# First pass over a graph's matrix: rows read in quarters and turned in place by VectorE, in place of a turned copy kept in HBM

## The chip, the cores and the metric

The kernel runs on one core of one Trainium2 chip. The metric is the device time of one execution in microseconds (us). All arithmetic is fp32, apart from one product that the kernel before does in two fp32r pieces.

## What is computed

`adj` is a 5120 x 5120 fp32 matrix A (105 MB), `x` a 5120 x 64 fp32 matrix. Cut to what matters:

```python
e  = par0 * par1 * (diag[:, None] * x @ W) + x          # W, diag, par: first 2048 rows / other 3072 rows
h  = A @ (A.T @ e)                                       # layer 0: one product with A.T, one with A
x0 = layernorm(x + layernorm(h) * gamma + beta + x)
x1 = layernorm(x0 + (1 - 0.1 * x0 - 0.01 * sum(x0 * (A @ x0))))          # layer 1
deg = clip(rowsum(A) + 1, 1)                                              # layer 2
z  = concat([x1, (A @ x1 + x1) / deg]) @ W2 + b2;  x2 = layernorm(x1 + relu(z) / norm(relu(z)))
t1 = A @ x2;  t2 = 2 * A @ t1 - x2;  t3 = 2 * A @ t2 - t1                 # layer 3
out = layernorm(x2 + x2 @ W3[0] + t1 @ W3[1] + t2 @ W3[2] + t3 @ W3[3] + b3)
```

So there is one product with the transposed matrix (u = A.T e) and six with A itself (h, layer 1, layer 2, t1, t2, t3), each of 64 columns. A does not fit in the on-chip memory (SBUF); each product streams blocks of it.

## The kernel before, in words

A is cut into 10 x 10 blocks of 512 x 512 (1 MB each; `BLK`, `NB`). TensorE contracts over partitions. A product with A.T can use a block as it lies in HBM (128 rows of A on the partitions, four such tiles to a block); a product with A needs the block turned.

**First stage (L501 to L561 on TensorE, L433 to L453 on ScalarE, L768 to L796 on VectorE).** For each block column j, SyncE loads the ten blocks (i, j) as they lie (`load`, L342; five buffers `nat`; runs of 512 elements, 2 KB). TensorE turns each block with 16 transposes (L539), ScalarE copies the four results from PSUM into `at_raw` (L447) and stores the turned block to a scratch tensor in HBM, `a_transposed` (L430, one megabyte, 8 KB to a partition). TensorE adds the block's part of u (L551, eight matmul records of 64 columns a block) and, one block column late, the block's part of h: ScalarE rounds the turned block to fp32r (`at_hi`, L425), VectorE forms the rest (`at_lo`, L740), and TensorE multiplies both with the split u (L509). VectorE adds up the rows of each natural block for `deg` (L765) and the parts of h into `part` (L751). So when the first stage ends, u and nearly all of h are there, and 100 MB have been read and 100 MB written.

**The sweeps (`multiply_block`, L621 to L665).** The five other products run as "sweeps" s = 0 to 4, with 5 for the tail (`SWEEPS = 6`). The rows of a product can be finished in one order and the next product started in the other, so that one loaded block serves the end of product s-1 and the beginning of product s at once: `BOTH` blocks have 128 columns of weights, two vectors side by side; `BEGIN` and `END` blocks 64 columns for one of the two. The list `blocks` holds 332 of them: 55 BEGIN in sweep 0; 42 BOTH, 13 BEGIN and 3 END under each of sweeps 1 to 4; 45 END in the tail. The last block column of h comes between the stage and sweep 0, in `last_h_part` (L667). Sixteen slots hold turned blocks (`at_raw` 10, `at_more` 6); a plan made when the program is built gives each block a slot, and SyncE issues the 291 loads (L378) in order, each behind a wait for the block that last used its slot. TensorE's order is written out: between the halves of a block (`mid`) it turns the finished rows back (`turn`, L576), after VectorE has added PSUM to `part` (`add_y`, L975); VectorE then does the row's norm and so on (`end_l1` and so on), with one power function by GpSimd in each norm (L396).

**Order on the queues.** SyncE issues the loads in the order of use, and the stores of the output at the end. VectorE, ScalarE and TensorE each follow a list by hand; what an engine waits for holds up all that stands behind it on that engine.

What changes in the kernel stands in these functions:

Of the kernel before, what the change touches and what calls it, by code (L numbers as in the profile page):

```python
# [6 lines left out]
F32R = mybir.dt.float32r  # L29
# [9 lines left out]
def build(nc, x, adj, w_u, diag_u, par_u, w_i, diag_i, par_i, gamma, beta, l2_w, l2_b, l3_w, l3_b, out):  # L39
# [7 lines left out]
    MORE = 6  # L47
    SWEEPS = 6
# [3 lines left out]
    SLOW_ENDS = (1, 2)  # L52
    QUICK_ENDS = (3, 4)
    REACH = 12
    HOLD, HELD = (3, 5), 3
    HT = TB // 2
    NAT = 5
    BLOCKS = NB * NB
    assert NB % NAT == 0 and NB % 2 == 0
# [4 lines left out]
    x_rows = x.rearrange("(t p) f -> p t f", p=P)  # L64
    out_rows = out.rearrange("(t p) f -> p t f", p=P)

    ctx = ExitStack()
    with ctx:
# [9 lines left out]

        at_raw = sb("at_raw", [P, NB, TB, BLK])
        rows = sb("rows", [P, NT, F])  # L80


# [3 lines left out]
        u_split = sb("u_split", [P, TB, 2, F], F32R)  # L86
        u_turned = sb("u_turned", [P, BLK])
        x_turned = u_turned[0:F, :]
# [11 lines left out]

# [8 lines left out]

        with nc.sbuf_tensor("at_hi", [P, 2 * 2, HT, BLK], F32R) as at_hi, \  # L110
                nc.sbuf_tensor("at_lo", [P, 2 * 2, HT, BLK], F32R) as at_lo, \
                nc.sbuf_tensor("nat", [P, NAT, TB, BLK], F32) as nat, \
                nc.sbuf_tensor("e", [P, NT, F], F32) as e_rows:
            pass

        OVER_HALVES = 4
        at_more = sb("at_more", [P, MORE, TB, BLK])
        vectors = sb("vectors", [P, NT, 2, F])  # L120
        base = sb("base", [P, NT, F])

        u_last = tc

        ps_t = [pb(f"ps_turn{k}") for k in range(TB)]
        ps_u = pb("ps_u")
        ps_h = [pb(f"ps_h{k}") for k in range(2)]
        ps_back = pb("ps_back")
        back = ps_back[:, 0:TB * F].rearrange("p (t f) -> p t f", t=TB)

        ps_both = [ps_u, ps_back]
        ps_own = [ps_h, [ps_u, ps_t[2]]]

        yw = [[ps_t[n][:, k * TB * F:(k + 1) * TB * F].rearrange("p (t f) -> p t f", t=TB) for k in range(2)]
              for n in range(2)]

        ps_xt = ps_t[3]
        xw = ps_t[2][:, :].rearrange("p (t f) -> p t f", t=TB)  # L140

        ps_xt_in = ps_h[0]
        xw_in = ps_h[1][:, 0:TB * F].rearrange("p (t f) -> p t f", t=TB)
# [11 lines left out]
        nat_loaded = [sem(f"nat_loaded{k}") for k in range(NAT)]  # L155
        nat_summed = sem("nat_summed")
        u_added = sem("u_added")
        u_copied = sem("u_copied")
        u_back = sem("u_back")
        u_ready = sem("u_ready")  # L160
        turned = sem("turned")
        at_evacuated = sem("at_evacuated")
        at_stored = [sem(f"at_stored{k}") for k in range(NB)]
        hi_ready = sem("hi_ready")
        lo_ready = sem("lo_ready")
        multiplied = sem("multiplied")
        h_free = sem("h_free")
        last_h_done = sem("last_h_done")
        hy_ready = sem("hy_ready")
        raw_loaded = [sem(f"raw_loaded{k}") for k in range(NB + MORE)]  # L170
# [13 lines left out]
        N_CONSTS, N_WEIGHTS = 6, 16  # L184
        N_ROOTS = 6 * NB
        BASES = (1, 2)

# [7 lines left out]
        BOTH, END, BEGIN = range(3)  # L195
        blocks = []


# [3 lines left out]
        def then(what, s, r, where=None):  # L202
            after.setdefault(len(blocks), []).append((what, s, r))
            if where is not None:
                where.setdefault(len(blocks), []).append((what, s, r))

        for s in range(SWEEPS):
# [6 lines left out]
            if s == 0:  # L214
                for r in range(NB - 1):
                    blocks += [(s, r, q, BEGIN) for q in range(r + 1)]
                    then("keep", s, r)
                blocks += [(s, NB - 1, q, BEGIN) for q in range(NB - 1)]
            else:


# [34 lines left out]


# [20 lines left out]


        group = [("own" if which == BEGIN else "both", s, r) for s, r, q, which in blocks]  # L280
# [6 lines left out]

# [8 lines left out]
        spans, span_of = [[(i, NB - 1), []] for i in range(NB)], []  # L296
        for b, (s, r, q, which) in enumerate(blocks):
            key = at(s, r), at(s, q)
            found = [n for n in range(len(spans)) if spans[n][0] == key
                     and (n < NB and not spans[n][1]  # L300
                          or spans[n][1] and (b - spans[n][1][-1] <= REACH or s in HOLD and q < r <= HELD))]
            if found:
                spans[found[-1]][1].append(b)
                span_of.append(found[-1])
            else:
                span_of.append(len(spans))
                spans.append([key, [b]])

        last_use = [spans[i][1][-1] for i in range(NB)] + [-1] * OVER_HALVES \
            + [-2] * (MORE - OVER_HALVES)  # L310
        uses = [1 if n < NB else 0 for n in range(NB + MORE)]
        slot_of = list(range(NB))
        loads = []
        load_no = [0] * NB
        for key, its in spans[NB:]:
            slot = min(range(NB + MORE), key=lambda n: last_use[n])
            assert last_use[slot] < its[0]
            slot_of.append(slot)
            loads.append((key, slot, last_use[slot], uses[slot] == 0))
            load_no.append(sum(1 for l in loads if l[1] == slot))  # L320
            last_use[slot] = its[-1]
            uses[slot] += 1

        def raw(slot):
            return at_raw[:, slot] if slot < NB else at_more[:, slot - NB]
# [8 lines left out]

        @block.sync
        def _(sp):
            sp.dma_start(rows[:, 0:TB, :], x_rows[:, 0:TB, :]).then_inc(x_first_loaded, 16)
# [4 lines left out]
            def load(j, i):  # L342
                n = NB * j + i

                if not (isinstance(j, int) and j == 0 and i < NAT):
                    sp.wait_ge(u_added, n - NAT + 1)
                    sp.wait_ge(nat_summed, n - NAT + 1)
                sp.dma_start(nat[:, i % NAT], a_blocks[:, i * TB:(i + 1) * TB, bass.ds(j * BLK, BLK)])\
                    .then_inc(nat_loaded[i % NAT], 16)

            for i in range(NB):
                load(0, i)
                if i == 0:
                    sp.dma_start(rows[:, TB:NT, :], x_rows[:, TB:NT, :]).then_inc(x_loaded, 16)
            with sp.Fori(1, NB) as j:
                for i in range(NB):
                    load(j, i)
            columns_there = [0] * NB
            for (i, j), slot, b, first in loads:
                if columns_there[i] <= j:  # L360

                    sp.wait_ge(at_stored[i], 16 * (j + 1))
                    columns_there[i] = j + 1
                if not first:
                    sp.wait_ge(block_done, b + 1)
                    if slot < NB and columns_there[slot] < NB:

                        sp.wait_ge(at_stored[slot], 16 * NB)
                        columns_there[slot] = NB
                elif slot < NB + OVER_HALVES:  # L370

                    sp.wait_ge(multiplied, 2 * (BLOCKS - NB) + 4)
                else:

                    n_last = BLOCKS - NAT + slot - NB - OVER_HALVES
                    sp.wait_ge(u_added, n_last + 1)
                    sp.wait_ge(nat_summed, n_last + 1)
                sp.dma_start(raw(slot).rearrange("p t n -> p (t n)"), at_dram[i, j])\  # L378
                    .then_inc(raw_loaded[slot], 16)
            for r in range(NB):  # L380
                sp.wait_ge(out_ready, r + 1)
                i = at(SWEEPS - 1, r)
                sp.dma_start(out_rows[:, i * TB:(i + 1) * TB, :], rows[:, i * TB:(i + 1) * TB, :])\
                    .then_inc(stored, 16)
            sp.wait_ge(stored, 16 * NB)
# [14 lines left out]
        def _(act):  # L400
            def const(dst, src, loaded=consts_loaded):
                act.dma_start(dst, src).then_inc(loaded, 16)

            const(diag_flat[0:UT, :], diag_u.rearrange("(t p) -> t p", p=P))
            const(diag_flat[UT:NT, :], diag_i.rearrange("(t p) -> t p", p=P))
            const(w0[:, 0, :], w_u)

# [7 lines left out]
            for h in range(2):  # L415
                half = slice(h * F, (h + 1) * F)
                const(twice[half, 0, :], l2_w[F:2 * F, :], weights_loaded)
                for k in range(1, 4):
                    const(twice[half, k, :], l3_w[k], weights_loaded)
# [625 lines left out]
```

## Time and profile before

| | |
|---|---|
| time, median of 2 runs | 1672.88 us (1672.71 to 1673.04) |
| span of the profiled execution (first to last instruction) | 1666.0 us |
| so outside the span | some 6.9 us |
| TensorE / weight loads / VectorE / ScalarE busy | 1605.0 / 828.1 / 776.5 / 420.1 us |
| HBM read and written | 411.69 MB and 106.17 MB |

A matmul record's duration is its latency: records overlap, and the time that one takes from the engine is the group's busy time divided by its count. A 512-column fp32 matmul of the code appears as two records. "DMA share" is the mean busy share of the core's 16 DMA engines; it can come out a little above 1. PEclk is the granted TensorE clock as a share of full speed.

### The profile page before, as it was taken

How to read it: one execution, taken by the hardware profiler on the slowest of the kernel's cores; microseconds unless marked ns; L12 is line 12 of the kernel's file. 1: busy time of each engine (PE TensorE's matmuls, PEld its weight loads, DVE VectorE, ACT ScalarE, POOL GpSimd, SP SyncE). 2: the span in 40 equal slices, each digit the busy share in tenths (PEclk: the TensorE clock that was granted, in tenths of full speed). 3: DMA queues.
4: the chain of work that ended last, by engine and by line, in shares of the span. 5: the costliest groups of instructions: out<-in, count | busy, mean ns of one | idle time of the engine just before them, and what ended most of it. 6: DMA issues, size and time to landing. Idle time of an engine off the chain costs nothing.

```text
span 1666.0 us, 20499 instructions
## 1 busy us (share of the span) xinstructions
PE 1605.0 (96%) x6938; PEld 828.1 (50%) x6938; DVE 776.5 (47%) x1334; ACT 420.1 (25%) x651; POOL 61.6 (4%) x66
## 2 busy tenths in 40 slices
PE   7999999999999999999999989999999999999998
PEld 5656666665665653333444434444444444444433
DVE  5788888888888887423321243222210011100232
ACT  2466666666666650000000000000000000000000
POOL 0000000000000002100000010000000000000010
PEclk9999999999999999999999999999999999999999
DMA  9999999999999987999788757787278866888896
GB/s 322 410 363 336 336 347 343 332 350 337 339 352 334 333 301 286 420 421 408 256 287 291 277 204 276 282 290 286 77 268 289 312 240 256 301 313 292 325 402 263
DMA packets 118187, 518.63 MB, mean 311 GB/s; under 512 B 15692, under 2 KB 16884, under 8 KB 68084
## 3 DMA queue, kind: packets, MB, share of 16 engines
q1 hardware_dynamic: 102048, 412.66, 67.7%
q10 hardware_dynamic: 16084, 105.23, 16.6%
q8 instruction: 36, 0.59, 0.1%
q14 instruction: 19, 0.16, 0.0%
HBM read 411.69 MB, written 106.17 MB: 311 GB/s over the span
## 4 chain that ended last, share of the span: by engine, by line
issue 99%; POOLq 0%; POOL 0%; DVE 0%
POOL power_out L396 0%; POOLq L394 0%; POOLq L396 0%; DVE rows L840 0%; POOL ident L389 0%; POOLq L391 0%; POOL ident L391 0%; POOLq L1035 0%
## 5 line engine op out<-in xcount | busy, mean ns | idle before, releaser
L447 ACT ACTIVATE at_raw<-ps_turn 128x512 f32<-128x512 f32 x400 | 206.6, 604 | 214.4 <-DVE at_lo L740 189.0
L664 PE MATMUL ps_back<-at_raw,vectors 128*128 128x512 f32 (+1 forms) x592 | 242.4, 596 | 1.0 <-DVE part L985 1.0
L765 DVE TENSOR_REDUCE row_part<-nat 128x2048 f32 (+1 forms) x100 | 228.1, 2281 | 1.0 <-issue 0.2
L664 PE MATMUL ps_u<-at_raw,vectors 128*128 128x512 f32 (+1 forms) x648 | 223.5, 600 | 3.2 <-DVE part L996 3.2
L539 PE MATMUL ps_turn<-ident,nat 128*128 128x128 f32 x1600 | 200.8, 279 | 20.4 <-ACT at_raw L447 10.3
L740 DVE TENSOR_TENSOR at_lo<-at_raw,at_hi 128x1024 fp32r<-128x1024 f32 x180 | 211.7, 1218 | 0.2 <-ACT at_hi L425 0.2
L539 PEld LDWEIGHTS ps_turn<-ident,nat 128*128 128x128 f32 x1600 | 176.2, 141 | 52.9 <-ACT at_raw L447 37.2
L551 PE MATMUL ps_u<-nat,e 128*64 128x512 f32 x800 | 193.7, 605 | 0.0
L425 ACT ACTIVATE at_hi<-at_raw 128x1024 fp32r<-128x1024 f32 x180 | 182.2, 1076 | 8.9 <-PE ps_h L509 8.2
L664 PE MATMUL ps_back<-at_more,vectors 128*128 128x512 f32 (+1 forms) x408 | 160.3, 595 | 0.0
L461 ACT ACTIVATE part<-ps_h 128x512 f32<-128x512 f32 x40 | 23.9, 597 | 540.7 <-PE ps_h L664 540.7
L664 PEld LDWEIGHTS ps_back<-at_raw,vectors 128*128 128x128 f32 (+1 forms) x592 | 95.4, 179 | 124.4 <-issue 124.1
L509 PE MATMUL ps_h<-at_hi,u_split 128*128 128x512 f32 x360 | 150.6, 418 | 0.0
L509 PE MATMUL ps_h<-at_lo,u_split 128*128 128x512 f32 x360 | 142.1, 395 | 0.0
L664 PEld LDWEIGHTS ps_u<-at_raw,vectors 128*128 128x128 f32 (+1 forms) x648 | 82.0, 164 | 119.7 <-issue 118.6
L664 PE MATMUL ps_u<-at_more,vectors 128*128 128x512 f32 (+1 forms) x352 | 139.0, 595 | 0.0
L396 POOL TENSOR_TENSOR power_out<-power_in,minus_half 128x4 f32<-128x4 f32 x60 | 60.9, 1015 | 1600.7 <-DVEq L802 1600.7
L509 PEld LDWEIGHTS ps_h<-at_hi,u_split 128*128 128x128 f32 x360 | 67.5, 187 | 78.1 <-DVE at_lo L740 36.5
L664 PEld LDWEIGHTS ps_back<-at_more,vectors 128*128 128x128 f32 (+1 forms) x408 | 63.0, 175 | 84.8 <-issue 84.3
L751 DVE TENSOR_TENSOR part<-part,ps_h 128x512 f32<-128x512 f32 x90 | 61.8, 687 | 75.1 <-PE ps_h L509 75.1
L664 PEld LDWEIGHTS ps_u<-at_more,vectors 128*128 128x128 f32 (+1 forms) x352 | 54.3, 176 | 72.8 <-issue 72.6
L985 DVE TENSOR_TENSOR part<-part,ps_back 64x512 f32<-64x512 f32 (+1 forms) x25 | 17.1, 686 | 145.4 <-PE ps_back L664 144.9
(100 smaller groups left out, 935.3 us busy)
## 6 DMA issues: line engine op xcount, KB each, us to landing
at_raw<-a_transposed SPq DMA_DIRECT2D x170, 1024.0 KB, 5.3
at_more<-a_transposed SPq DMA_DIRECT2D x121, 1024.0 KB, 5.4
nat<-in_adj SPq DMA_DIRECT2D x100, 1024.0 KB, 6.0
a_transposed<-at_raw ACTq DMA_DIRECT2D x100, 1024.0 KB, 4.3
out<-rows SPq DMA_DIRECT2D x10, 128.0 KB, 3.5
rows<-in_x SPq DMA_DIRECT2D x1, 128.0 KB, 2.4
twice<-in_L_gnn_weight ACTq DMA_DIRECT2D x6, 16.0 KB, 6.1
vec<-in_L_gnn_ln_gamma ACTq DMA_DIRECT2D x1, 32.0 KB, 5.5
```

The source lines that it names most:

```text
L396: nc.gpsimd.tensor_tensor(power_out[:, :], power_in[:, :], minus_half[:, :], ALU.pow)\
L425: nc.scalar.activation(at_hi[:, 2 * slot + h], at_raw[:, raw, h * HT:(h + 1) * HT], ACT.Copy).then_inc(hi_ready, 1)
L447: nc.scalar.activation(at_raw[:, i, t, :], ps_t[t][:, :], ACT.Copy)\
L461: nc.scalar.activation(part[:, i * BLK:(i + 1) * BLK], ps_own[s == 0][r % 2][:, :], ACT.Copy).then_inc(own_copied, 1)
L509: mm = pe.matmul(acc[:, :], left[:, t].rearrange("p h f -> p (h f)"), half[:, 2 * slot + t // HT, t % HT, :], start=start and t == 0 and h ...
L539: mm = pe.transpose(ps_t[t][:, c * P:(c + 1) * P], nat[:, i % NAT, c, t * P:(t + 1) * P], ident[:, :])
L551: mm = pe.matmul(ps_u[side, :], e_rows[:, i * TB + c, :], nat[:, i % NAT, c, :], start=i == 0 and c < 2, stop=i == NB - 1 and c >= TB - 2)
L664: mm = pe.matmul(acc, left, tiles[:, t, :], start=first, stop=last)
L740: V.tensor_tensor(at_lo[:, 2 * slot + h], at_raw[:, raw, h * HT:(h + 1) * HT], at_hi[:, 2 * slot + h].bitcast(F32), ALU.subtract).then_inc ...
L751: V.tensor_tensor(part[:, cols], part[:, cols], ps_h[i % 2][:, :], ALU.add).then_inc(h_free, 1)
L765: V.reduce_sum(row_part[:, i * TB:(i + 1) * TB, bass.ds(j, 1)].rearrange("p t o -> p (t o)"), nat[:, i % NAT], AX.X).then_inc(nat_summed, 1)
L985: V.tensor_tensor(part[parts, cols], part[parts, cols], ps_both[r % 2][parts, :], ALU.add)\
```

## The change

- **No turned copy in HBM.** The scratch tensor, TensorE's 1600 transposes, ScalarE's 400 copies, the 100 stores, the split of the turned blocks into `at_hi` and `at_lo` and the fp32r product are gone. A is read again from `adj` for every use.
- **Rows renumbered.** A row index is i (block), a (quarter, 0 to 3), c (tile, 0 to 3), y (0 to 31): partition a*32 + y of tile c. So every load is four DMAs of 32 partitions each, one for each quarter a of the partitions. `x`, `diag` and `out` are read and written in the same order.
- **First pass by rows (`NAT` blocks).** For block column k, the ten blocks (i, k) are loaded as they lie (`adj_rows`: runs of 512 elements, 2 KB) and TensorE adds u_k from them. Behind each block column k > 0 come k BEGIN blocks of h from turned blocks. Their rest comes behind block column 9.
- **Turned blocks.** A turned block is loaded with `adj_quarters`: partition a*32 + y gets, for each of 16 groups b of 32 rows, the 128 elements of quarter a in row (b, y): 16 runs of 128 elements (512 bytes) to a partition. Then one VectorE instruction transposes all 32 x 32 squares of the [128 x 2048] slot in place (`V.transpose`, `turn_next`), and TensorE reads the slot through a strided pattern.
- **h is a sweep like the others**: `SWEEPS = 7`. The list has 490 blocks: 100 NAT, 210 BOTH, 120 BEGIN, 60 END. Sweep 0 has the 100 NAT and 55 BEGIN blocks; five sweeps (1 to 5) have 42 BOTH, 13 BEGIN and 3 END blocks each; 45 END blocks end it.
- **Slots**: 16 for both kinds; a plan picks the slot whose block is used again last, among those last used at least `APART` = 6 blocks back. It gives 423 loads: 100 natural, 323 turned (55 in sweep 0, 39 to 46 where a later sweep's blocks stand, 44 in the tail). For 245 of the loads the wait on SyncE ends 5 blocks before the block that needs it.
- **SyncE issues all four quarters of each block**, in the order 0, 2, 1, 3. ScalarE's list has no loads of A.
- **Row sums**: each natural block is summed half by VectorE (`V.reduce_sum` over two of the four tiles) and half by ScalarE (two activations with `accum_out`).
- **VectorE's order**: a block's transpose is placed three blocks ahead of the block (`LEAD = 3`), or earlier inside the waits of a row's end (`turn_spare`).

The core of the diff:

```diff
-    MORE = 6
-    SWEEPS = 6
+    Q = 4
+    QP = P // Q
+    SLOTS = 16
+    APART = 6
+    SWEEPS = 7
+    LEAD = 3
+    SUM_LEAD = 2
...
-    at_dram = nc.dram_tensor("a_transposed", [NB, NB, P, TB * BLK], F32, kind="Internal").ap()
-    a_blocks = adj.rearrange("(t p) j -> p t j", p=P)
+    adj_rows = adj.rearrange("(i a c y) j -> i a y c j", a=Q, c=TB, y=QP)
+    adj_quarters = adj.rearrange("(i b y) (j a w) -> i j a y b w", b=BLK // QP, y=QP, a=Q, w=P)
...
+        for k in range(NB):
+            for i in range(NB):
+                blocks += [(0, k, i, NAT)]
...
+            then("u", 0, k, mid)
+            if k > 0:
+                blocks += [(0, k - 1, q, BEGIN) for q in range(k)]
+                then("keep", 0, k - 1)
...
+        def load_quarters(eng, n, quarters):
+
+            need, slot, _, _, free_at = loads[n]
+            if free_at > 0:
+                eng.wait_ge(block_done, free_at)
+                if free_at - 1 in sum_no:
+                    eng.wait_ge(summed_dve, sum_no[free_at - 1] + 1)
+                    eng.wait_ge(summed_act, sum_no[free_at - 1] + 1)
+            for a in quarters:
+                if need[0] == "rows":
+                    dst = blk[quarter(a), slot].rearrange("p (c j) -> p c j", c=TB)
+                    src = adj_rows[need[1], a, :, :, need[2] * BLK:(need[2] + 1) * BLK]
+                else:
+                    dst = blk[quarter(a), slot].rearrange("p (b w) -> p b w", w=P)
+                    src = adj_quarters[need[1], need[2], a]
+                eng.dma_start(dst, src).then_inc(loaded[slot], 16)
...
+            for n in range(len(loads)):
+                load_quarters(sp, n, (0, 2, 1, 3))
...
             def multiply_block(b):
...
+                pe.wait_ge(turned, turn_no[load_of[b]] + 1)
...
+                tiles = blk[:, slot_of[b]].rearrange("p (a d c y) -> p c d a y", a=Q, d=TB, c=TB)
...
+            def sum_rows(b):
+
+                n = load_of[b]
+                s, k, i, _ = blocks[b]
+                dve.wait_ge(loaded[loads[n][1]], n_loaded(n))
+                V.reduce_sum(row_part[:, i * TB + HT:(i + 1) * TB, k],
+                             blk[:, loads[n][1], HT * BLK:].rearrange("p (t j) -> p t j", t=HT),
+                             AX.X).then_inc(summed_dve, 1)
...
+            def turn_next():
+
+                n = to_turn[n_done[0]]
+                slot = loads[n][1]
+                dve.wait_ge(loaded[slot], n_loaded(n))
+                V.transpose(blk[:, slot], blk[:, slot]).then_inc(turned, 1)
+                n_done[0] += 1
```

## Rows read from the trace of the kernel before

**Rows 1.** The page: busy time of each engine, and 40 equal slices.

```profile
PE 1605.0 (96%) x6938; PEld 828.1 (50%) x6938; DVE 776.5 (47%) x1334; ACT 420.1 (25%) x651; POOL 61.6 (4%) x66
...
PE   7999999999999999999999989999999999999998
PEld 5656666665665653333444434444444444444433
DVE  5788888888888887423321243222210011100232
ACT  2466666666666650000000000000000000000000
```

**Rows 2.** Busy time by stage: window, its length, PE, PEld, DVE, ACT, POOL (instructions), PEclk, DMA share, GB/s.

```profile
35.00:60.00 25.00, 25.00 (x174) 16.95 (x173) 18.63 (x20) 9.50 (x19) 0.00 (x0) 1.00 1.03 410
60.00:625.00 565.00, 542.75 (x3009) 343.22 (x3008) 482.61 (x393) 359.45 (x546) 0.00 (x0) 1.00 0.94 342
...
636.00:755.00 119.00, 119.00 (x570) 43.49 (x566) 53.34 (x236) 5.66 (x10) 18.18 (x18) 0.99 0.93 379
...
955.00:1155.00 200.00, 194.66 (x633) 90.15 (x634) 66.05 (x219) 10.86 (x19) 19.19 (x19) 0.98 0.73 264
1155.00:1355.00 200.00, 195.11 (x636) 90.47 (x635) 24.25 (x57) 7.15 (x12) 2.02 (x2) 0.99 0.68 244
...
1555.00:1666.00 111.00, 100.69 (x486) 39.51 (x484) 33.52 (x134) 1.19 (x2) 10.10 (x10) 0.99 0.86 333
```

**Rows 3.** Groups of instructions by form: line engine op, shapes, count, busy us, mean ns, idle before.

```profile
L664 PE MATMUL ps_back<-at_raw,vectors 128*128 128x512 f32 x472 | 214.3, 597 | 0.0
L740 DVE TENSOR_TENSOR at_lo<-at_raw,at_hi 128x1024 fp32r<-128x1024 f32 x180 | 211.7, 1218 | 0.2 <-ACT at_hi L425 0.2
L447 ACT ACTIVATE at_raw<-ps_turn 128x512 f32<-128x512 f32 x400 | 206.6, 604 | 214.4 <-DVE at_lo L740 189.0 <-PE ps_turn L539 25.4
L539 PE MATMUL ps_turn<-ident,nat 128*128 128x128 f32 x1600 | 200.8, 279 | 20.4 <-ACT at_raw L447 10.3 <-DVE u_split L711 10.1
...
L765 DVE TENSOR_REDUCE row_part<-nat 128x2048 f32 x80 | 182.4, 2280 | 0.0
...
L664 PE MATMUL ps_u<-at_raw,vectors 128*64 128x512 f32 x328 | 78.8, 603 | 3.2 <-DVE part L996 3.2
```

**Rows 4.** The page: DMA queues, and issues with size and time to landing.

```profile
q1 hardware_dynamic: 102048, 412.66, 67.7%
q10 hardware_dynamic: 16084, 105.23, 16.6%
...
at_raw<-a_transposed SPq DMA_DIRECT2D x170, 1024.0 KB, 5.3
...
nat<-in_adj SPq DMA_DIRECT2D x100, 1024.0 KB, 6.0
```

**Rows 5.** Windows 10 to 12 us and 700 to 740 us, columns as in rows 2.

```profile
10.00:12.00 2.00, 0.24 (x2) 0.05 (x1) 0.85 (x2) 0.00 (x0) 0.00 (x0) 1.00 1.12 220
700.00:740.00 40.00, 40.00 (x194) 14.35 (x192) 12.23 (x56) 1.79 (x3) 4.04 (x4) 1.00 1.01 420
```

**Rows 6.** SyncE's issues in order of time: start us, us, line.

```profile
2.88 0.58 SPq L348 DMA_DIRECT2D nat<-in_adj  x1
3.68 0.81 SPq L354 DMA_DIRECT2D rows<-in_x  x1
4.53 6.72 SPq L348 DMA_DIRECT2D nat<-in_adj  x1
```

**Rows 7.** A window in which TensorE fell short, columns as in rows 2.

```profile
765.00:770.00 5.00, 5.00 (x16) 1.35 (x14) 3.64 (x17) 0.60 (x1) 1.01 (x1) 0.60 1.01 421
```

More of the change, by code:

```diff
@@ L183, in build @@
         block = ctx.enter_context(nc.Block())
-        N_CONSTS, N_WEIGHTS = 6, 16
+        N_CONSTS, N_WEIGHTS = 4 + NB, 16
         N_ROOTS = 6 * NB
-        BASES = (1, 2)
+        BASES = (2, 3)
         def at(s, r):
             return NB - 1 - r if s % 2 == 0 else r
-        BOTH, END, BEGIN = range(3)
+        BOTH, END, BEGIN, NAT = range(4)
         blocks = []
@@ L276, in build @@
                     events.append(("base", s, r))
-        group = [("own" if which == BEGIN else "both", s, r) for s, r, q, which in blocks]
+        group = [("u", s, r) if which == NAT else ("own" if which == BEGIN else "both", s, r)
+                 for s, r, q, which in blocks]
         def opens(b):
@@ L309, in build @@
[L309 to L322, printed above, removed]
@@ L324, in raw @@
-        def raw(slot):
-            return at_raw[:, slot] if slot < NB else at_more[:, slot - NB]
+        needs = [("rows", q, at(s, r)) if which == NAT else ("turned", at(s, r), at(s, q))
+                 for s, r, q, which in blocks]
+        never = len(blocks)
+        again, seen = [never] * len(blocks), {}
+        for b in range(len(blocks) - 1, -1, -1):
+            again[b] = seen.get(needs[b], never)
+            seen[needs[b]] = b
+        holds = [None] * SLOTS
+        loads, slot_of, load_of = [], [], []
@@ new lines, in build @@
+        n_in_slot = [0] * SLOTS
+        for b, need in enumerate(needs):
+            here = [n for n in range(SLOTS) if holds[n] is not None and holds[n][0] == need]
+            if here:
+                n = here[0]
+                load_of.append(holds[n][1])
+            else:
+                empty = [n for n in range(SLOTS) if holds[n] is None]
+                if empty:
+                    n, free_at = empty[0], 0
+                else:
+                    n = max((n for n in range(SLOTS) if holds[n][2] <= b - APART),
+                            key=lambda n: (again[holds[n][2]], -holds[n][2]))
+                    free_at = holds[n][2] + 1
+                n_in_slot[n] += 1
+                load_of.append(len(loads))
+                loads.append((need, n, n_in_slot[n], b, free_at))
+            slot_of.append(n)
+            holds[n] = (need, load_of[b], b)
@@ new lines, in build, with n_loaded @@
+        begin_at = [max(free_at for _, _, _, _, free_at in loads[:n + 1]) for n in range(len(loads))]
+        turn_no, n_turned = {}, 0
+        for n, (need, _, _, _, _) in enumerate(loads):
+            if need[0] == "turned":
+                turn_no[n] = n_turned
+                n_turned += 1
+        row_blocks = [b for b in range(len(blocks)) if blocks[b][3] == NAT]
+        sum_no = {b: k for k, b in enumerate(row_blocks)}
+        def n_loaded(n):
+            return 16 * Q * loads[n][2]
@@ L340, in _ @@
                 sp.dma_start(dst, src).then_inc(consts_loaded, 16)
[L342 to L379, printed above, removed]
@@ new lines, in _, with turn_due @@
+            to_turn = sorted(turn_no)
+            n_done = [0]
+            def turn_next():
[4 more added lines that the diff above has]
+                n_done[0] += 1
+            def turn_due(b):
+                while n_done[0] < len(to_turn):
+                    n = to_turn[n_done[0]]
+                    if max(loads[n][3] - LEAD, begin_at[n]) > b:
+                        break
+                    turn_next()
@@ L798, in _, with turn_spare @@
+            def turn_spare(b):
+                if n_done[0] < len(to_turn):
+                    n = to_turn[n_done[0]]
+                    if begin_at[n] <= b and loads[n][3] - LEAD - 1 <= b:
+                        turn_next()
             roots = [0]
@@ L904, in end_l2 @@
                 root = ask_power()
[L905 to L906 removed]
+                meanwhile()
                 dve.wait_ge(pow_ready, root)
```

566 lines of the change are left out of this document (224 added, 342 removed).

## The prediction

> **What bounds the kernel now.** I read the page's busy times and slices first, then the windows by stage, then the groups by form, then the DMA queues. TensorE is busy in 96% of the span and VectorE in 47% [rows 1]; since matmul records overlap, that alone says little, so I looked for stages in which something else is full as well. There are four [rows 2]. (1) To 636 us, the first stage: TensorE busy 542.75 of 565 us, VectorE 482.61, DMA share 0.94 at 342 GB/s. TensorE and the DMA engines are both nearly full, and what fills TensorE here is 1600 transposes and the fp32r product. (2) 636 to 755 us, sweep 0 and the ends of layer 0: TensorE busy throughout, but loads at full share; 700 to 740 us is at share 1.01 and 420 GB/s [rows 5]. The loads set this stage. (3) Sweeps 1 to 4, 755 to 1555 us, 200 us each: TensorE busy 195 of 200 us, DMA share 0.68 to 0.73, VectorE 24 to 66 us [rows 2]. TensorE alone. (4) The tail, 111 us.
>
> What TensorE needs for a block comes from the forms [rows 3]: a 128-column record takes 214.3/472 = 0.454 us, eight to a BOTH block, 3.63 us; a 64-column one takes 78.8/328 = 0.240 us, 1.92 us for a BEGIN, END or NAT block. Check on a sweep: 42 x 3.63 + 16 x 1.92 = 183 us, and with the turns of rows 200 us.
>
> **TensorE, VectorE and ScalarE after the change.** TensorE loses 200.8 us of transposes [rows 3] and the fp32r product, and gets one more sweep, 200 us [rows 2]. VectorE loses L740 (211.7 us) and half of the row sums; it gets 323 transposes of 128 x 2048. The trace has no transpose. The nearest row is the reduction over the same 128 x 2048, 2.28 us [rows 3], 0.9 elements a ns in each partition; bounds are 1.2 us (L740 moves 1024 elements in 1.218 us and could not be beaten by more than a doubled rate) and twice 2.28, 4.6 us. I take 2.28: 45 in a sweep make 103 us, beside the 24 to 66 us that VectorE has there now, so up to 170 of 200 us. That lies beside TensorE's work. Queued behind a transpose that waits for its load are the adds and norms on which TensorE's turns wait; LEAD = 3 blocks, 11 us of TensorE's time, covers it, and I put 3 us a sweep on it. ScalarE loses 206.6 us of copies and gets 200 half sums at 0.604 us, 121 us: no cost. The wait of a natural slot for both sums lies inside the five blocks of lead: no cost; without the lead it would be 1 us a block, 100 us in all. GpSimd's power functions are unchanged.
>
> **The transfers, which decide.** Bytes fall: 391 loads (100 natural, 291 turned) and 100 stores of a megabyte (1.049 MB), 412.66 and 105.23 MB on the two queues [rows 4], become 423 loads, 444 MB. But each turned load is 2048 runs of 512 bytes in place of 8 KB runs, and every DMA covers 32 partitions.
> - Natural blocks, 2 KB runs: at 35 to 60 us, such loads and the stores together move 410 GB/s [rows 2]: 2.56 us a block.
> - Turned blocks, 512-byte runs: no row. Bounds: 2 KB runs from above, 410 GB/s; from below, the load of x in 256-byte runs, alone in the window at 10 to 12 us, 220 GB/s at full share [rows 5]. Per run on one of 16 engines these are 79.9 ns and 18.6 ns. I draw a line through both (9.8 ns and 0.0342 ns a byte): 512 bytes take 27.4 ns, 299 GB/s, 3.5 us a block; the bounds are 2.56 and 4.77 us.
> - Quarters: all large DMAs of this trace cover 128 partitions, so nothing shows what one over 32 does. If 16 engines that all write the same quarter of the partitions can write only at half the rate, a block takes 1.049/210 = 5.0 us (half of 420 [rows 5]); if engines drift apart or the hardware buffers enough, it takes what the runs allow. One queue hands every engine the quarters in the same order, so nothing but drift puts two engines on different quarters. I take something between: 3.8 us for a turned block and 3.2 us for a natural one. The turned one suffers less, since its short runs leave an engine idle at 299 of 420 GB/s anyway. This is a choice, and the weakest term of the sum.
> - Issue: a 512-run DMA took SyncE 0.58 us [rows 6]; the four quarters of a turned block have 512 runs each, 2.3 us. Under 3.8 us a block, so hidden, but not by much; the 6.72 us of the next issue [rows 6] is a queue that was full behind x, so SyncE also stalls when the DMA engines are behind, which costs nothing by itself.
>
> The Trainium skill, "SBUF — State Buffer", in "Door 1: The DMA port swizzle" and the section on two DMAs for both halves, speaks against this change: partitions 0 to 63 and 64 to 127 lie behind eight ports each, a DMA over 32 partitions reaches eight, and two DMAs on both halves gained only 6% over one (196 GB/s measured for 64 partitions). By it 444 MB at 208 GB/s would take 2132 us, an estimate from that page; no row here bears on it, and it names the mechanism of the second rival below. The other way, "DMA: Bandwidth & Descriptors", Specifications, puts the least size for line rate at 512 bytes; by that a turned block would cost 2.56 us and the sum below would be 1531 us. The row at 256 bytes lies below that limit, so it does not contradict the rule; I give it little, because 2 KB runs with 410 are already under the 420 of 8 KB runs.
>
> **The sum**, against the profiled execution of 1666.0 us. Start until the blocks flow, 9 us (x is 1.3 MB in short runs, 6 us at 220 GB/s, from 3 us on [rows 5, 6]). Sweep 0, set by loads: 100 x 3.2 + 55 x 3.8 = 529 us; TensorE needs only 155 x 1.92 = 298 us of it. Five sweeps: 45 loads x 3.8 = 171 us, under TensorE's 200 us, so 5 x (200 + 3) = 1015 us. Tail: 44 loads x 3.8 = 167 us, TensorE 86 us, and 5 us for the last row's end. Together 9 + 529 + 1015 + 172 = 1725 us, against 1666. The before column in the same terms: 636 + 119 + 4 x 200 + 111. So 755 us of the first stage and sweep 0 become 538 + 200 (one more sweep) + 15, about even, and the tail, where loads bound, loses 61 us. With the 6.9 us that the runs show over the span, **1732 us**, 3.5% slower.
>
> **Rivals.**
> 1. *Quarters cost nothing.* Engines drift apart within a few blocks and the runs alone set the rate. 9 + 256 + 193 + 1000 + 154 + 5 = 1617, with 6.9: 1624 us, 2.9% faster. It decides from a turned block at 3.5 us and a natural one at 2.56 us; the change is faster than before up to about 3.65 and 2.9. For it: full share is kept for tens of us in the trace without any help [rows 5]. Against it: those DMAs cover all partitions.
> 2. *Engines stay in step, half rate.* 5.0 us a block: sweep 0 takes 155 x 5 = 775 us; a sweep 45 x 5 = 225 us, now set by loads; the tail 225 us: 9 + 775 + 1125 + 225 + 7 = 2141 us. For it: one queue, one order. Against: it needs 1700 DMAs without drift. Half drift, 4.25 and 3.75 us, gives 609 + 1025 + 192 + 16 = 1842 us.
> 3. *VectorE becomes the bound*, a transpose at 4.6 us: 45 x 4.6 + 45 = 252 us a sweep, and 9 + 529 + 1260 + 207 + 7 = 2012 us. For it: nothing in the trace; against: L740 and L765 both move 0.84 to 0.9 elements a ns [rows 3].
> 4. *The clock.* TensorE needs 298 of 529 us in sweep 0. Where it fell short of blocks before, the granted clock was 0.60 for 5 us [rows 7], the lower of its two levels (1.2 GHz in place of 2.4) for most of it. If that held all through sweep 0, its blocks would need 596 us, 67 more than the loads: 1799 us. Against: that dip is short, and the mean of the load-bound stage around it is 0.99 [rows 2].
>
> **How the numbers follow.** Forecast (a block between 3.65 and 4.25 us turned): 0.45, of which 0.18 within 2% and 0.27 slower. Rival 1: 0.27 (0.04 of it with 512-byte runs at the full rate). Rival 2: 0.15. Rival 3: 0.05; rival 4: 0.08. A measurement tells about 2%: faster is under 1639 us, slower over 1706 us. So faster 0.27, same 0.18, slower 0.15 + 0.27 + 0.13 = 0.55. The range, 1595 to 1980 us, leaves out rival 2 at its full size and the fastest part of rival 1; the forecast's own is 1640 to 1850 us.
>
> **What would show it.** In the windows of sweep 0: DMA share near 1 at 270 to 310 GB/s and a block each 3.2 to 3.8 us; TensorE's idle time there ended by VectorE's transposes and by DMAs; under rival 1 320 GB/s or more, under rival 2 about 210 GB/s at a share near 1. Sweeps 1 to 5: 200 to 205 us each, TensorE full; transposes of 2.28 us, 323 of them. The tail about 170 us. Wrong would be: sweeps much longer than 200 us, sweep 0 under 460 or over 610 us, SyncE solid with issues while the DMA share is low, or transposes over 3 us.

## The result, and the profile after

The changed kernel takes 2199.08 us (2190.56 to 2207.6, two runs) against 1672.88 us: 1.317 times as long (95% interval 1.308 to 1.325). I had forecast 1732 us in a range of 1595 to 1980 us. The direction was right and the size was far off. The total lies near that of my second rival (2141 us), engines of one queue that stay in step, but that is luck in part: it had 775 us for sweep 0, 1125 for the five sweeps and 225 for the tail, where 711, 1303 and 174 were measured, and a part of the five sweeps is one that no rival had. One of the four executions of each of q9 and q12 below (1851 and 1881 us) fell in a slower state of the chip, and it is left out of their ratios to the kernel before.

The page of the changed kernel: busy times, slices, queues, and the groups that answer to [rows 1, 3, 4].

```profile
PE 1613.8 (74%) x5002; PEld 660.4 (30%) x5002; DVE 1145.6 (52%) x1382; ACT 181.8 (8%) x481; POOL 61.3 (3%) x66
...
DMA  9999999999999899979999699985999969999999
GB/s 213 244 244 244 248 248 230 225 226 233 230 224 225 160 195 184 212 143 173 182 197 206 125 201 176 210 162 106 202 179 189 201 125 223 222 222 224 239 268 219
...
q1 hardware_dynamic: 745844, 445.00, 102.9%
...
L621 DVE STREAM_TRANSPOSE blk<-blk 128x2048 f32<-128x2048 f32 x323 | 743.8, 2308 | 556.3 <-DMA blk<-in_adj 546.9
...
L525 PE MATMUL ps_both<-blk,base 128*64 128x512 f32 x800 | 237.4, 728 | 123.3 <-DMA blk<-in_adj 119.1
```

Fewer bytes move than before (445 MB on one queue against 412.66 and 105.23 MB [rows 4]), and yet that queue's packets fill the DMA engines nearly all the time: in sweep 0 the share is full at 225 to 248 GB/s, where full share was 410 to 420 GB/s before [rows 2, 5]. The transposes take 2.31 us each, as the forecast had it. VectorE's wait of 546.9 us for loads in front of them is the new fact.

By stage (window, length, PE, PEld, DVE, ACT, POOL, PEclk, DMA share, GB/s). From the second row on, the marks are the times at which the records of the block products reach 1240 (sweep 0 done), then 464 more a sweep; the first row is a window inside sweep 0, and the last two look into the last sweep:

```profile
100.00:600.00 500.00, 280.08 (x966) 79.79 (x964) 182.89 (x129) 105.80 (x313) 0.00 (x0) 0.77 1.11 237
711.00:973.00 262.00, 212.94 (x546) 91.17 (x544) 167.02 (x311) 5.97 (x10) 19.78 (x20) 0.89 0.99 187
973.00:1240.00 267.00, 225.04 (x655) 100.20 (x652) 164.89 (x248) 11.28 (x19) 10.53 (x11) 0.89 0.96 181
1240.00:1506.00 266.00, 223.40 (x666) 100.94 (x664) 167.81 (x263) 11.87 (x20) 19.19 (x19) 0.90 0.92 174
1506.00:1780.00 274.00, 224.47 (x636) 103.36 (x636) 127.83 (x97) 6.56 (x11) 1.01 (x1) 0.86 0.93 176
1780.00:2014.00 234.00, 211.38 (x628) 96.96 (x626) 120.61 (x83) 5.97 (x10) 0.00 (x0) 0.91 1.11 203
2014.00:2188.00 174.00, 107.77 (x442) 41.74 (x438) 123.13 (x171) 0.60 (x1) 10.11 (x10) 0.78 1.14 242
...
1780.00:1820.00 40.00, 38.53 (x149) 16.99 (x146) 13.91 (x15) 2.39 (x4) 0.00 (x0) 0.87 0.57 109
1820.00:2000.00 180.00, 165.72 (x456) 75.63 (x454) 99.38 (x61) 3.58 (x6) 0.00 (x0) 0.94 1.22 222
```

Against the terms of the sum: sweep 0 ends at 711 us where 538 was forecast (the load-bound stage at 237 GB/s, TensorE's need of 298 us far below it); the five sweeps take 1303 us where 1015 was forecast; the tail 174 where 172 was. Two terms failed, then, by 173 and 288 us. The tail held by two errors that cancel: its blocks took 4.3 us and not 3.8, but only some 40 of the 44 loads fell into it (242 GB/s over 174 us are 42 MB).

### The profile page after: what moved, and what is told of

It reads as the page before. It is cut to its first block, busy times and chain, and to the rows that moved or that the text cites. A ratio compares the mean times of both kernels' runs of the same rounds, so it can differ in the third digit from the quotient of the medians.

```text
span 2188.8 us, 15525 instructions
## 1 busy us (share of the span) xinstructions
PE 1613.8 (74%) x5002; PEld 660.4 (30%) x5002; DVE 1145.6 (52%) x1382; ACT 181.8 (8%) x481; POOL 61.3 (3%) x66
## 4 chain that ended last, share of the span: by engine, by line
issue 99%; POOLq 0%; POOL 0%; DVE 0%
POOL power_out L355 0%; POOLq L353 0%; POOLq L355 0%; DVE rows L678 0%; POOL ident L348 0%; POOLq L350 0%; POOL ident L350 0%; POOLq L885 0%
## 5 line engine op out<-in xcount | busy, mean ns | idle before, releaser
L621 DVE STREAM_TRANSPOSE blk<-blk 128x2048 f32<-128x2048 f32 x323 | 743.8, 2308 | 556.3 <-DMA blk<-in_adj 546.9
L566 PE MATMUL ps_both<-blk,vectors 128*128 128x512 f32 (+1 forms) x2160 | 935.7, 647 | 108.4 <-DVE part L827 86.8
L566 PEld LDWEIGHTS ps_both<-blk,vectors 128*128 128x128 f32 (+1 forms) x2160 | 366.2, 192 | 611.6 <-issue 478.3
L566 PE MATMUL ps_own<-blk,vectors 128*64 128x512 f32 x960 | 271.8, 707 | 81.3 <-DVE blk L621 76.0
L525 PE MATMUL ps_both<-blk,base 128*64 128x512 f32 x800 | 237.4, 728 | 123.3 <-DMA blk<-in_adj 119.1
L609 DVE TENSOR_REDUCE row_part<-blk 128x2 f32<-128x1024 f32 x100 | 121.7, 1218 | 232.9 <-DMA blk<-in_adj 231.4
L389 ACT ACTIVATE junk<-blk 128x512 f32<-128x512 f32 x200 | 124.2, 622 | 456.3 <-DMA blk<-in_adj 456.3
L566 PEld LDWEIGHTS ps_own<-blk,vectors 128*64 128x64 f32 x960 | 70.6, 157 | 254.5 <-issue 142.4
L355 POOL TENSOR_TENSOR power_out<-power_in,minus_half 128x4 f32<-128x4 f32 x60 | 60.6, 1010 | 2123.4 <-DVEq L643 2123.4
L482 PE MATMUL ps_y<-ident,part 128*128 128x64 f32 x320 | 59.7, 349 | 76.0 <-DVE part L816 75.3
L482 PE MATMUL ps_y<-twice,part 128*128 128x64 f32 x320 | 58.5, 344 | 73.2 <-DVE part L816 72.3
```

The lines of the kernel that those rows point to most:

```text
L355: nc.gpsimd.tensor_tensor(power_out[:, :], power_in[:, :], minus_half[:, :], ALU.pow)\
L389: add = nc.scalar.activation(junk[:, c], blk[:, loads[n][1], c * BLK:(c + 1) * BLK], ACT.Copy, accum_out=row_part[:, i * TB + c, k:k + 1])
L482: mm = pe.matmul(yw[n % 2][k][:, t, :], part[:, i * BLK + t * P:i * BLK + (t + 1) * P], weights, start=True, stop=True)
L525: mm = pe.matmul(ps_both[k % 2][half(t), :], e_rows[:, i * TB + t, :], tiles[:, t], start=i == 0 and t < 2, stop=i == NB - 1 and t >= TB - 2)
L566: mm = pe.matmul(acc, left, tiles[:, t], start=first, stop=last)
L609: V.reduce_sum(row_part[:, i * TB + HT:(i + 1) * TB, k], blk[:, loads[n][1], HT * BLK:].rearrange("p (t j) -> p t j", t=HT), AX.X).then_in ...
```

## Experiments

All stand beside the kernel before, measured again on their chip at 1665 to 1671 us. Edits are to the changed kernel. q1, q9 and q12 were timed four times, the others once. Where a kernel was timed more than once its executions lie up to 0.9% apart, those two aside, so differences of 2% and more are clear of that.

### Which quarters are in flight together

`q1_two_queues_halves`, and `q2_two_queues_same_half` with (0, 2) and (1, 3):

```diff
-                load_quarters(sp, n, (0, 2, 1, 3))
+                load_quarters(sp, n, (0, 1))
...
-                    pass
+                    load_quarters(act, next_load, (2, 3))
```

> The changed kernel, but SyncE issues quarters 0 and 1 of each block (partitions 0 to 63) and ScalarE quarters 2 and 3 (64 to 127). Theory A (the DMA engines work through one queue in step, so that at any time all write the same half of the partitions, at half rate): with two queues each engine alternates between the halves, sweep 0 moves over 290 GB/s in place of 230, takes some 480 to 540 us in place of 711, and the whole is 1620 to 1750 us. Theory B (512-byte runs and many small DMAs are slow as such, the quarters don't matter): bytes, runs and DMAs are the same, so the rate stays at 220 to 240 GB/s and the time at 2150 to 2250 us. Theory C (SyncE's issuing is the limit): the same gain as A, since two engines issue.

> Two queues again, but SyncE issues quarters 0 then 2 and ScalarE 1 then 3, so that both queues are on the same half of the partitions at about the same time. A: as one queue, 2000 to 2200 us, unless the two queues drift apart. C: as with the two queues split by halves, under 1750 us. B: 2150 to 2250 us.

`q3_order_0123` is `load_quarters(sp, n, (0, 1, 2, 3))`:

> SyncE alone, quarters in the order 0, 1, 2, 3: two quarters of the same half follow each other. If drift or buffering already evened out part of the conflict in the order 0, 2, 1, 3 (the form of A that my forecast used), this is slower by 3% or more, up to 218 GB/s or less in sweep 0. If engines are fully in step, or under B and C, the same within 2%.

`q4_all_partitions` (blocks are read from wrong rows of A and from other parts of it, so the products are of other matrices; work and bytes are the same, in a quarter as many DMAs):

```diff
+    adj_flat = adj.rearrange("(t p) j -> p t j", p=P)
...
-            return 16 * Q * loads[n][2]
+            return 16 * loads[n][2]
...
+            if need[0] == "rows":
+                dst = blk[:, slot].rearrange("p (c j) -> p c j", c=TB)
+                src = adj_flat[:, need[1] * TB:(need[1] + 1) * TB, need[2] * BLK:(need[2] + 1) * BLK]
+                eng.dma_start(dst, src).then_inc(loaded[slot], 16)
+            else:
+                dst = blk[:, slot].rearrange("p (b w) -> p b w", w=P)
+                top, left = min(need[1] * BLK, N - 16 * P), need[2] * BLK + need[1] % Q * P
+                src = adj[top:top + 16 * P, left:left + P].rearrange("(b p) w -> p b w", p=P)
+                eng.dma_start(dst, src).then_inc(loaded[slot], 16)
```

> SyncE alone, but one DMA over all 128 partitions for each block in place of four over 32: the same bytes and the same runs (2 KB and 512 bytes), read from other places of A where they must be, so the kernel computes with wrongly placed rows and other parts of A. A: the runs alone set the rate, 299 GB/s for turned blocks (27 ns a run on an engine) and 410 for natural ones; about 1620 us. B: 2150 us or more. C (a quarter of the issues): about 1620 us too. This measures the cost of a 512-byte run by itself.

Measured: two queues split by halves 1946.42 us (1.167 times before, 1.162 to 1.171); two queues on the same half 2258.79 us; one queue in order 0, 1, 2, 3 2305.48 us; one queue, all partitions 1797.87 us. A window inside sweep 0 of each, in that order, from the four traces:

```profile
100.00:500.00 400.00, 240.49 (x968) 74.51 (x964) 187.08 (x130) 114.61 (x340) 0.00 (x0) 0.84 1.07 301
```

```profile
100.00:500.00 400.00, 216.55 (x736) 62.48 (x732) 140.28 (x101) 99.06 (x294) 0.00 (x0) 0.75 1.11 231
```

```profile
100.00:500.00 400.00, 217.32 (x722) 60.40 (x718) 134.22 (x98) 86.40 (x256) 0.00 (x0) 0.75 1.10 224
```

```profile
100.00:400.00 300.00, 197.76 (x790) 64.88 (x792) 156.21 (x108) 84.45 (x250) 0.00 (x0) 0.81 1.05 327
```

The share is full in all four; the rate is 301, 231, 224 and 327 GB/s. The four windows don't hold quite the same mix of blocks, but the whole of sweep 0 does, and it says the same: 4.5 us a block with all quarters on one queue in the order 0, 2, 1, 3, 3.6 with two queues by halves, 3.2 with all partitions. Queues and issuing engines don't matter (231 with two queues on the same half, 224 to 237 with one): theory C falls. Bytes and runs don't either, as they are the same in the first three: B falls. What matters is which quarters are in flight together, as A says. That it is the written halves of the partitions is A's explanation, and these runs don't separate it from one other: a quarter of the partitions is also a fixed quarter of the block's rows or columns in HBM, so each order of writes is an order of reads too. A in its strict form gets the order wrong: 0, 1, 2, 3 is 5% slower than 0, 2, 1, 3, and the changed kernel's 237 GB/s lies above the 210 of strict halving. So there is drift or buffering between quarters, as the forecast supposed, but it gives back a quarter of the loss (27 of the 117 GB/s between 210 and 327), where my values had three quarters.

A's times were misses all the same: 1620 to 1750 us for q1, 1620 us for q4 and 2000 to 2200 us for q2, measured 1946, 1798 and 2259; and q3 was to move 218 GB/s or less in sweep 0 if the order mattered, measured 224. In q1 and q4 sweep 0 was somewhat over what was expected (563 us against 480 to 540 in q1; 510 in q4); the five sweeps were far over it, and they are the subject of the next part.

What the runs' length does to this can be read where one kind of block is loaded alone. Windows inside sweep 0 with next to nothing but natural blocks, 2 KB runs: the changed kernel, then all partitions:

```profile
72.00:96.00 24.00, 14.70 (x62) 3.89 (x60) 7.76 (x7) 7.69 (x24) 0.00 (x0) 0.96 1.06 246
```

```profile
74.00:96.00 22.00, 20.55 (x98) 7.02 (x96) 13.24 (x12) 10.70 (x32) 0.00 (x0) 1.00 1.05 387
```

Turned blocks, 512-byte runs, in the last sweep: 222 GB/s in the changed kernel (its row is above), then order 0, 1, 2, 3, two queues by halves, and all partitions:

```profile
1900.00:2090.00 190.00, 167.21 (x456) 77.22 (x456) 102.73 (x64) 3.58 (x6) 0.00 (x0) 0.91 1.22 215
```

```profile
1620.00:1780.00 160.00, 154.48 (x438) 71.71 (x438) 99.53 (x62) 2.99 (x5) 0.00 (x0) 0.98 1.20 288
```

```profile
1480.00:1640.00 160.00, 159.55 (x456) 73.54 (x456) 98.04 (x63) 3.58 (x6) 0.00 (x0) 0.98 1.18 290
```

And turned blocks in the tail, for the changed kernel (2050 to 2150 us) and for all partitions (1660 to 1760 us):

```profile
2050.00:2150.00 100.00, 64.75 (x262) 24.21 (x258) 69.39 (x78) 0.00 (x0) 4.04 (x4) 0.80 1.21 262
```

```profile
1660.00:1760.00 100.00, 72.85 (x292) 28.03 (x290) 84.86 (x119) 0.00 (x0) 7.07 (x7) 0.81 1.15 289
```

290 GB/s is the price of 512-byte runs by themselves: 3.6 us a block, against 3.5 from the line drawn through the rows at 256 bytes and 2 KB. On one queue, quarters take 23% from it (222 GB/s, 4.7 us a block) and 36% from 2 KB runs (246 in place of 387 GB/s, 4.3 us in place of 2.7), so the long runs suffer more, and both kinds end near the same rate. Two queues by halves give 512-byte runs all of it back (288). In the tail the changed kernel moves 262 GB/s (4.0 us a block), a loss of only 9%; why it is faster there than in the last sweep with the same kind of block is open.

### Why the sweeps take over 200 us

With loads over all partitions, the sweeps still took 1134 us (510 to 1643), at a DMA share of 0.77 in the second one:

```profile
737.00:974.00 237.00, 216.83 (x656) 96.92 (x654) 165.44 (x250) 11.28 (x19) 10.59 (x11) 0.92 0.77 204
```

So loads had room in that sweep. What TensorE waited for in that kernel (released by VectorE's add; us in total, times, longest us), at the weight loads and at the products of a row's turn:

```profile
PEld ps_y L485 <- DVE part L819: 124.5, 45, 11.8
PE ps_y L485 <- DVE part L819: 87.6, 36, 11.0
```

and, in order of time, VectorE in the changed kernel as a row ends (start us, us, engine line, operands, idle before and its releaser):

```profile
1104.17 2.31 DVE L621 STREAM_TRANSPOSE blk<-blk 128x2048 f32<-128x2048 f32 x1 [2.34 <-DMA blk<-in_adj]
1106.41 0.64 DVE L827 TENSOR_TENSOR part<-part,ps_both 64x512 f32<-64x512 f32 x1
...
1107.20 3.04 PE L566 MATMUL ps_both<-blk,vectors 128*128 128x512 f32 x4 [4.38 <-DVE part L827]
...
1108.82 2.31 DVE L621 STREAM_TRANSPOSE blk<-blk 128x2048 f32<-128x2048 f32 x1 [1.77 <-DMA blk<-in_adj]
1111.16 0.69 DVE L816 TENSOR_TENSOR part<-part,ps_both 64x512 f32<-64x512 f32 x1
...
1111.91 1.97 PE L482 MATMUL ps_y<-ident,part 128*128 128x64 f32 x8 [1.67 <-DVE part L816]
```

TensorE has finished its row and needs 0.64 us of VectorE; VectorE stands at a transpose of a block up to three ahead and waits for its load. The transpose ends, the add follows, and TensorE has waited 4.38 us. The next add is behind another transpose again. `q5_row_work_first` changes that order alone, on the kernel with all partitions (other parts of A, as there):

```diff
             for b in range(len(blocks) + 1):
-                turn_due(b)
                 for what, s, r in after.get(b, ()):
...
+                turn_due(b)
```

> The kernel with one DMA over 128 partitions for each block (wrongly placed rows and other parts of A, as in q4_all_partitions, 1798 us), with VectorE's order changed: the adds and the row work of a step stand before the transposes placed at that step, not behind them. There the five sweeps took 205 to 237 us each, not 200. Theory D (TensorE's turns of rows wait for adds that are queued behind a transpose that waits for its load): sweeps go down by 10 us or more each, the whole to 1700 to 1760 us. Theory E (the sweeps are short of loads: 512-byte runs and five blocks of lead): no change within 1%, or slower because transposes come later.

`q6_no_transposes` (unturned blocks multiplied) and, with natural reads for all blocks (other parts of A), `q7_long_runs` and `q8_long_runs_no_transposes`:

```diff
-                pe.wait_ge(turned, turn_no[load_of[b]] + 1)
+                pe.wait_ge(loaded[slot_of[b]], n_loaded(load_of[b]))
...
-            to_turn = sorted(turn_no)
+            to_turn = []
```

> As q4_all_partitions, but the transposes are left out and TensorE waits for the load itself (so it multiplies unturned blocks). D: sweeps back to about 200 us, the whole 1640 to 1680 us. E: sweeps still 220 us or more, over 1740 us. The difference to q5_row_work_first is what the transposes' own time and latency cost.

> As q4_all_partitions, but blocks to be turned are read like natural ones, in 2 KB runs (so other parts of A); transposes stay. It prices the 512-byte runs: loads at 2.6 to 2.9 us in place of 3.6 to 4.1. If the sweeps are set by loads (E) they fall to about 200 us and the whole to about 1560 us; if by VectorE's order (D), the first stage and the tail gain some 80 us together and the sweeps stay over 215 us: 1650 to 1710 us.

> 2 KB runs over all partitions and no transposes (unturned blocks multiplied, other parts of A): what is left is TensorE's work and the plain loads. Both theories: sweeps at about 200 us, sweep 0 at some 420 us, tail at 115 us, the whole 1530 to 1570 us. If it is more, something that I have not named (the slots, SyncE's waits, the clock) costs time too.

| us | whole | sweep 0 ends | five sweeps | tail |
|---|---|---|---|---|
| forecast | 1732 | 538 | 1015 | 172 |
| changed kernel | 2199 | 711 | 1303 | 174 |
| two queues by halves (q1) | 1946 | 563 | 1233 | 149 |
| all partitions (q4) | 1798 | 510 | 1134 | 153 |
| and row work first (q5) | 1707 | 492 | 1065 | 148 |
| q4 without transposes (q6) | 1638 | 488 | 1011 | 136 |
| q4 with 2 KB runs (q7) | 1695 | 471 | 1071 | 151 |
| q7 without transposes (q8) | 1551 | 440 | 1010 | 100 |

The order is worth 91 us, 68 of it in the sweeps, and the transposes altogether 160 us (122 in the sweeps): D. In the same sweep of the kernel without transposes (q6) the 237 us are 206, with the same loads at a higher share, and the granted clock is 0.99 in place of 0.92:

```profile
689.00:895.00 206.00, 201.88 (x654) 92.30 (x650) 57.71 (x200) 11.29 (x19) 10.11 (x10) 0.99 0.91 235
```

The new order does not end the wait; in q5 the products of a row's turn still wait for the add, 51.8 us in place of 87.6. What the transposes cost beyond the order, 70 us of which 54 are in the sweeps, was not taken apart:

```profile
PE ps_y L485 <- DVE part L819: 51.8, 22, 7.6
```

E gets a part as well, against my reading of it as a rival: with long runs the sweeps fall by 63 us while the transposes stay, though without transposes run length changes nothing in them (1011 and 1010). That would fit D, as a faster load shortens VectorE's wait for it. q8, at 1551 us, came out inside its 1530 to 1570, though with sweep 0 at 440 us where some 420 were expected and the tail at 100 in place of 115; its sweeps, 202 us each, leave nothing unnamed there. q6, at 1638 us, lies just under its 1640 to 1680. In q8 2 KB runs move 387 GB/s all through sweep 0, 2.7 us a block and not the 2.56 that I had taken from the 410 GB/s of loads and stores together:

```profile
50.00:430.00 380.00, 288.11 (x1254) 83.31 (x1252) 126.39 (x123) 121.98 (x362) 0.00 (x0) 1.00 1.05 387
```

### Both causes in the whole kernel

`q9_two_queues_row_work_first` is q1 with the order of q5, `q10_one_queue_row_work_first` the changed kernel with that order alone; `q11_two_queues_lead5` and `q12_two_queues_lead2` are q9 with `LEAD = 5` and `LEAD = 2`.

> The whole computation: two queues split by halves (q1_two_queues_halves, 1946 us), and VectorE's row work before the transposes of the same step. If both causes add up, the sweeps lose some 15 to 20 us each as they did with loads over all partitions (91 us in all): 1840 to 1880 us, still over the 1670 us of the kernel before, since quarters still cost 36 us in place of 27 ns a run... that is 36 ns in place of 27 to 32. If the order only helped because loads were fast there, 1930 us or more.

> The changed kernel with nothing but VectorE's order changed (row work of a step before its transposes); SyncE alone issues the quarters 0, 2, 1, 3. The part of the slowdown that is VectorE's order: 2100 to 2140 us if it is worth the same 91 us as beside fast loads; under 2080 us if it is worth more where loads come later, since each wait is longer; 2180 us or more if the loads' rate hides it.

> q9_two_queues_row_work_first with LEAD = 5 in place of 3, so that a step's transposes are those of blocks five ahead and VectorE waits for loads that have only just been issued. If a transpose in front of row work is what costs, this brings the cost back in part: 20 us or more slower than q9. If TensorE ever waited for transposes that came too late, it is faster.

> q9_two_queues_row_work_first (1807 us) with LEAD = 2: a transpose stands two blocks ahead of its use. With LEAD = 5 it took 2055 us, so VectorE's waits for loads in front of row work are dear. If some of that is left at 3: 1770 to 1800 us. If TensorE now waits for transposes that come too late (2.3 us each, two blocks are 3.8 to 7.3 us of TensorE's time): 1820 us or more.

| us | whole | sweep 0 ends | five sweeps |
|---|---|---|---|
| q10, one queue, row work first | 2074.10 | 685 | 1203 |
| q9, two queues, row work first | 1806.78 (1.082 of before; 1.075 to 1.089) | 546 | 1104 |
| q11, LEAD = 5 | 2054.95 | 589 | 1316 |
| q12, LEAD = 2 | 1834.87 (1.100; 1.094 to 1.107) | 550 | 1120 |

The order alone is worth 125 us with one queue and 140 us with two, more than the 91 us beside fast loads; q10 falls in the second of its three cases (worth more where loads come later), and q9 lies 33 us under its range, probably for the same reason. The 36 ns a run that q9's expectation names are those of quarters on one queue (222 GB/s); on two queues by halves the last sweep moved 288 GB/s, 28 ns a run. In q11 the five sweeps grow by 212 us. VectorE there, before the add of a row's end:

```profile
1181.58 2.31 DVE L621 STREAM_TRANSPOSE blk<-blk 128x2048 f32<-128x2048 f32 x1 [0.38 <-DMA blk<-in_adj]
1184.98 2.31 DVE L621 STREAM_TRANSPOSE blk<-blk 128x2048 f32<-128x2048 f32 x1 [1.09 <-DMA blk<-in_adj]
1190.12 2.31 DVE L621 STREAM_TRANSPOSE blk<-blk 128x2048 f32<-128x2048 f32 x1 [2.82 <-DMA blk<-in_adj]
1192.35 0.64 DVE L816 TENSOR_TENSOR part<-part,ps_both 64x512 f32<-64x512 f32 x1
```

A load may start five blocks ahead, so a transpose placed five ahead meets a load that has only just been issued, and the row's add waits for it. LEAD = 2 is slower than 3 by about 25 us (1826 to 1842 us against 1796 to 1810). What TensorE waited for (us in total, times, longest us), in q9 and in q12:

```profile
PE ps_y L482 <- DVE part L816: 69.3, 39, 7.6
...
PE ps_both L566 <- DVE blk L621: 22.4, 20, 6.0
```

```profile
PE ps_both L566 <- DVE blk L621: 78.5, 58, 6.3
...
PE ps_y L482 <- DVE part L816: 31.7, 29, 2.6
```

The wait for the row's add is halved, and the wait for the turned block (`blk`) more than triples: the transposes come too late. No version with the whole computation beat the kernel before; q9 is the best at 1807 us.

## Why the prediction was wrong, point by point

- **The stages of the kernel before, and TensorE's cost of a block**: right. 3.63 and 1.92 us a block give the 200 us a sweep that q6 and q8 show (1011 and 1010 us for five).
- **A transpose at 2.28 us**: right, 2.31. Rival 3, the same at 4.6 us, falls.
- **512-byte runs at 299 GB/s**: right, 290 GB/s in q4's last sweep. "DMA: Bandwidth & Descriptors" (the Trainium skill, Specifications) would have had line rate there; the run does not bear that out, with 387 GB/s for 2 KB runs beside it.
- **2 KB runs at 410 GB/s**: too high, 387. By the runs alone (the terms of rival 1) sweep 0 would have ended at 9 + 256 + 193 = 458 us; q4, without quarters, ended it at 510. So 52 of the 173 us by which sweep 0 missed its forecast are not the quarters'; VectorE's order has 18 of them (q5, 492).
- **Quarters at 3.8 and 3.2 us**: the first step that failed. A turned block took 4.7 us in the last sweep and a natural one 4.3; over sweep 0 it was (711 - 9)/155 = 4.5 us a block against (538 - 9)/155 = 3.4. I had taken a quarter of the loss of full halving for natural blocks and a fifth for turned ones, on the ground that engines would drift apart. The runs show most of the loss: 201 us of sweep 0 (711 - 510), where the sum had 80 (538 - 458). The step carried into the sweeps: the sum had 45 loads x 3.8 = 171 us under TensorE's 200, and with 4.7 us they are 212, over it. The last sweep shows it, at full share and 222 GB/s for all but its first 40 us. Of the 288 us that the five sweeps were over their forecast, the quarters cost 170 with the old order of VectorE's list (1303 - 1134) and 138 with the new one (1203 - 1065): more than the second step.
- **What the Trainium skill states.** That a DMA over part of the partitions has fewer ways into SBUF ("SBUF — State Buffer", Door 1, in the Trainium skill) agrees with the rates, 224 to 237 GB/s against 327; the ways themselves no run here shows. That two DMAs on both halves gain only 6% (the same page of the Trainium skill, the section on two DMAs for both halves) does not hold for this stream of 256 KB DMAs on two queues: it moved 301 in place of 237 GB/s, 27% more.
- **3 us a sweep for what is queued behind a waiting transpose**: the second step that failed. I wrote that LEAD = 3, 11 us of TensorE's time, covers it. The lead shortens TensorE's wait for a turned block. It does the reverse for the adds: it puts a wait for a load that is up to three blocks away in front of the work that TensorE needs now. The sweeps took 262 to 274 us (the last 234) in place of 203; the order alone gives back 125 us in all (q10), 100 of them in the sweeps. Another 54 us of the sweeps go with the transposes even when row work is first (q5 against q6), by a way that stays open.
- **Issue**: not a bound. Twice the issuers without both halves in flight (q2) gained nothing.
- **The clock** (rival 4): the granted clock was 0.77 of full speed in sweep 0, a mean between its two levels of 1.2 and 2.4 GHz, beside TensorE busy 280 of 500 us; so it did fall as TensorE waited. By the sum it can't have set the stage: at the lower level throughout, TensorE would have needed 596 us of the 702. In the sweeps it was 0.86 to 0.91 beside waits and 0.99 without them (q6), so it may have made the waits of the second cause somewhat dearer. How much, no run separates.
- **The range**: the two causes meet, since slower loads make VectorE's waits longer (the order is worth 91 us with loads over all partitions and 125 with quarters). I had let the halving rival stand at 0.15 and left its full size out of the range, and had no rival for the order of VectorE's list.

## What to carry to other kernels

A DMA that covers a fraction of the partitions should be judged by which others are in flight with it: put the two halves of the partitions on different queues, or cover all 128 in one, and don't count on one queue's order to mix them. When an in-order engine gets waits for loads, look at what stands behind each of them, and place the work that the bottleneck engine waits for in front; a longer lead is not safer if it moves the wait closer to the load's start. Judge both together: the same order of work cost 91 us with loads over all partitions and 125 with quarters.

## What had not been expected of the hardware

- One queue with 32-partition DMAs in the order 0, 2, 1, 3 moves 237 GB/s and in the order 0, 1, 2, 3 224 GB/s, both at full share; so the alternation of halves on one queue gives back only a little of what two queues give (301).
- The loss depends on the run: 36% with 2 KB runs alone (387 to 246 GB/s), 23% with 512-byte runs alone (290 to 222 GB/s, last sweep).
- DMA share reads "full" in all these cases, from 215 to 420 GB/s. It shows that the engines have packets to work on, not that they move bytes as fast as they could.
